# Cross-attention and a quantised FFN: keys from a transposed copy of the context, queries from a second layout of x normalised by ScalarE

## The reference

```python
def _L0_xattn_ref(Q, K, V):          # K = V = context, 16 heads of 16 columns
    q = Q.reshape(B, S, N_HEADS, D_K).transpose(0, 2, 1, 3)   # k and v likewise
    scores = jnp.einsum('bhqd,bhkd->bhqk', q, k) * scale      # scale = 1/4
    attn = jax.nn.softmax(scores, axis=-1)
    out = jnp.einsum('bhqk,bhkd->bhqd', attn, v)
    return out.transpose(0, 2, 1, 3).reshape(B, S, D_MODEL)
def fp4_linear(x, w):                # both quantised in blocks of 16, then x w^T
    return jnp.einsum('bsk,nk->bsn', fp4_quant_dequant(x), fp4_quant_dequant(w))
def _L0_ffn_ref(x, w_gate, w_up, w_down):
    h = jax.nn.silu(fp4_linear(x, w_gate)) * fp4_linear(x, w_up)
    return fp4_linear(h, w_down)
x = x + _L0_xattn_ref(_layernorm(x), ctx_1024, ctx_1024)
x = x + _L0_ffn_ref(_layernorm(x), L0_ffn_w_gate, L0_ffn_w_up, L0_ffn_w_down)
```

## Time and profile before

| | |
|---|---|
| time, 3 runs | median 542.06 us (539.32 to 543.23) |
| profiled execution | 543.02 us, span 541.2 us |
| busy | PE 498.4 (92%), PEld 398.7 (74%), DVE 453.1 (84%), ACT 360.9 (67%), POOL 270.0 (50%) |
| DMA | 40.63 MB, 75 GB/s on average |
| chain that ended last | PE 59%, DVE 21%, issue 11% |

### The profile page before, as it was taken

How to read it: one execution, slowest core, us unless ns; L and a number is a source line. 1 busy time by engine, 2 the same in 40 slices (tenths; PEclk the granted TensorE clock), 3 DMA queues, 4 the chain that set the end, 5 groups by cost and what they waited for, 6 DMA issues and landing times.

```text
span 541.2 us, 13897 instructions
## 1 busy us (share of the span) xinstructions
PE 498.4 (92%) x4105; PEld 398.7 (74%) x4132; DVE 453.1 (84%) x1175; ACT 360.9 (67%) x707; POOL 270.0 (50%) x391
## 2 busy tenths in 40 slices
PE   3788999999999999999886799999999999999996
PEld 2345666666666666655445699999999999999996
DVE  3688999999999999988554788888998888898764
ACT  3237888888888888877773456666566666656653
POOL 5214254445444345433415556676666666666543
PEclk9999999999999999999886899999999999999999
DMA  6758554454444554330000000000000000000000
GB/s 196 203 133 240 156 143 135 140 157 124 134 134 137 156 154 132 96 106 3 3 1 0 2 10 22 21 19 11 18 19 19 19 19 19 10 19 20 21 21 30
DMA packets 43799, 40.63 MB, mean 75 GB/s; under 512 B 4728, under 2 KB 43512, under 8 KB 43768
## 3 DMA queue, kind: packets, MB, share of 16 engines
q1 hardware_dynamic: 43768, 40.26, 26.2%
HBM read 10.55 MB, written 4.19 MB: 27 GB/s over the span
## 4 chain that ended last, share of the span: by engine, by line
PE 59%; DVE 21%; issue 11%; DMA 2%; POOL 2%; ACT 2%; DVEq 1%; SPq 0%; POOLq 0%; ACTq 0%
PE SC L1090 21%; DVE MF L682 12%; PE PV L1090 12%; PE MX L1023 4%; PE SC L1009 4%; PE PV L1041 4%; PE T L1115 4%; PE T L1120 2%; DVE stats L690 2%; DVE QN L703 2%; PE T L992 1%; DMA QS<-MT 1%; PE SC L1115 1%; PE T L955 1%; DVE MP L712 1%
## 5 line engine op out<-in xcount | busy, mean ns | idle before, releaser
L682 DVE TENSOR_REDUCE MF<-MX 128x2 f32<-128x512 f32 x256 | 167.5, 685 | 16.3 <-PE MX L1023 15.5
L535 ACT ACTIVATE P<-SC 128x512 f32<-128x512 f32 x256 | 142.7, 606 | 27.8 <-PE SC L1009 26.8
L1023 PE MATMUL MX<-KS,QS 96*128 96x256 bf16 x512 | 103.6, 287 | 6.7 <-DVE MF L682 2.9
L1009 PE MATMUL SC<-QS,KS 98*128 98x256 bf16 x512 | 100.2, 278 | 2.0 <-DMA QS<-MT 2.0
L484 POOL TENSOR_TENSOR HQ<-HN,hscale 128x704 f32<-128x704 f32 x31 | 43.2, 1393 | 61.4 <-DVE HN L839 61.4
L1041 PE MATMUL PV<-P,VA 128*32 128x256 f32 x1024 | 70.6, 394 | 2.7 <-ACT OT L544 0.8
L1009 PEld LDWEIGHTS SC<-QS,KS 98*128 98x128 bf16 x512 | 43.8, 98 | 36.3 <-ACT P L535 14.0
L614 ACT ACTIVATE HH<-T 128x768 fp32r<-128x768 f32 x31 | 25.2, 813 | 67.8 <-PE T L1115 67.8
L1090 PE MATMUL SC<-WH,XH 128*128 128x352 f32 x256 | 68.6, 350 | 0.0
L1023 PEld LDWEIGHTS MX<-KS,QS 96*128 96x128 bf16 x512 | 46.5, 100 | 29.3 <-DVE MF L682 19.0
L1090 PE MATMUL SC<-WH,XL 128*128 128x352 f32 x256 | 62.8, 327 | 0.0
(11 more groups left out here) (134 smaller groups left out, 1021.5 us busy)
## 6 DMA issues: line engine op xcount, KB each, us to landing
KS<-KP SPq DMA_DIRECT2D x96, 128.0 KB, 2.4
QS<-QP SPq DMA_DIRECT2D x96, 128.0 KB, 2.4
X<-in_x SPq DMA_DIRECT2D x16, 256.0 KB, 2.9
C<-in_ctx SPq DMA_DIRECT2D x16, 256.0 KB, 3.1
out<-OB SPq DMA_DIRECT2D x32, 128.0 KB, 1.7
W<-in_L_ffn_w_down SPq DMA_DIRECT2D x1, 704.0 KB, 5.7
W<-in_L_ffn_w_gate SPq DMA_DIRECT2D x1, 640.0 KB, 4.3
W<-in_L_ffn_w_up SPq DMA_DIRECT2D x1, 640.0 KB, 4.7
```

The lines of the kernel that those rows point to most:

```text
L535: nc.scalar.activation(P[g % 2][:, j, :, :], SC[h % 3][:, :, :], ACT.Exp, scale=0.25).then_inc(exp_done, 1)
L682: nc.vector.tensor_reduce(MF[st.slot(off, 2)][:, :, h:h + 1], MX[h % 2][:, :, :], AX.X, ALU.max, negate=True).then_inc(mx_done, 1)
L1009: last = nc.tensor.matmul(SC[h % 3][:, k, :], KS[r][0:ROWS, h, k * 128:(k + 1) * 128], QS[r][0:ROWS, h, :], start=True, stop=True)
L1023: last = nc.tensor.matmul(MX[h % 2][:, q, :], QS[r][0:PROD, h, q * 128:(q + 1) * 128], KS[r][0:PROD, h, :], start=True, stop=True)
```

## The change

Two further inputs are laid out before the launch: `x_p`, x with its columns by parity of the head, and `ctx_t`, the context transposed into the layout that the keys need. Both are loaded for each item beside x and the context (`load_first`), into rings of four buffers. The keys' parts no longer go through TensorE: ScalarE rounds the first part from the loaded tile, GpSimd subtracts it (KR), ScalarE rounds the second, GpSimd subtracts that and writes the third. The statistics are taken from the x_p tile, GpSimd makes a bias of mean and reciprocal root, and ScalarE normalises the tile in place with scale and bias. GpSimd's first work in a step is now the addition of the outputs to x. Many positions move.

```diff
-        QN = sb("QN", [128, QT, 2, DK, H // 2])
-        KN = sb("KN", [128, QT, 2, DK, H // 2])
+        QN = [sb(f"QN{r}", [128, QT, 2, DK, H // 2]) for r in range(RING)]
+        KT = [sb(f"KT{r}", [128, 512]) for r in range(RING)]
+        KR = sb("KR", [128, 512])
...
+            def load_first(b, r):
+                sp.dma_start(QN[r][:, :, :, :, :].rearrange("p q e d a -> p q (e d a)"),
+                             xp_d[:, bass.ds(b * QT, QT), :]).then_inc(first_loaded[r], 16)
+                sp.dma_start(KT[r][:, :], t_d[:, bass.ds(b, 1), :].rearrange("p a c -> p (a c)")).then_inc(first_loaded[r], 16)
+            def load_second(b, r):
+                sp.dma_start(C[r][:, :, :], c_d[:, bass.ds(b * QT, QT), :]).then_inc(loaded[r], 16)
...
                 for k_n, q_n, dst, parts, p, rows in ((1, 0, KS[0], KP[0], 0, (0, 3, 5)), (2, 0, KS[0], KP[0], 1, (1, 4)),
-                                                      (2, 1, QS[0], QP[0], 0, (0, 1, 2)), (3, 1, KS[0], KP[0], 2, (2,)),
+                                                      (3, 0, KS[0], KP[0], 2, (2,)), (3, 1, QS[0], QP[0], 0, (0, 1, 2)),
                                                       (3, 2, QS[0], QP[0], 1, (3, 4)), (3, 3, QS[0], QP[0], 2, (5,))):
-                    sp.wait_ge(k_out, k_n)
+                    sp.wait_ge(k_out if k_n < 3 else k_low, k_n if k_n < 3 else 1)
                     sp.wait_ge(q_out, q_n)
...
-            load(0, 0)
-            load(1, 1)
+            load_first(0, 0)
+            load_first(1, 1)
...
-            load(2, 2)
+            load_first(2, 2)
+            for b in range(2):
+                load_second(b, b)
...
-                    load(st.item(RING), st.slot(RING, RING))
+                    load_first(st.item(RING), st.slot(RING, RING))
+                    load_second(st.item(RING), st.slot(RING, RING))
                 if st.has(LEAD):
                     r = st.slot(LEAD, RING)
-                    sp.wait_ge(k_out, st.times(LEAD, 3, 3))
...
-                        load(3, 3)
+                        load_second(2, 2)
+                        load_first(3, 3)
                     if st.first == 2 - LEAD:
+                        load_second(3, 3)
...
-                if st.has(LEAD):
-                    r, rc = st.slot(LEAD, 2), st.slot(LEAD, RING)
-                    pool.wait_ge(loaded[rc], st.turn(LEAD, RING, 32))
-                    pool.wait_ge(k_tr, st.times(LEAD, 3))
-                    gate(pool)
-                    for q in range(QT):
-                        nc.gpsimd.tensor_scalar(KN[:, q, :, :, :], by_parity(C[rc][:, q, :]), 1.0, 0.0,
-                                                ALU.mult, ALU.add).then_inc(kn_ready, 1)
...
+                    r, rc = st.slot(LEAD, 2), st.slot(LEAD, RING)
+                    pool.wait_ge(k_out, st.times(LEAD, 2, 1))
+                    pool.wait_ge(k_low, st.times(LEAD, 1))
+                    gate(pool)
+                    nc.gpsimd.tensor_tensor(KR[:, :], KT[rc][:, :], KP[r][:, 0, :], ALU.subtract).then_inc(k_rest, 1)
+                if st.has(LEAD):
                     pool.wait_ge(stats_seq, st.times(LEAD, 4, 4))
                     gate(pool)
                     nc.gpsimd.tensor_scalar(ve[r][:, :], mv[:, :, 1], EPS, None, ALU.add).then_inc(ve_ready, 1)
-                    pool.wait_ge(ve_ready, st.times(LEAD, 1, 1))
+                    nc.gpsimd.tensor_scalar(nmean[:, :], mv[:, :, 0], -1.0, None, ALU.mult).then_inc(ve_ready, 1)
+                    pool.wait_ge(ve_ready, st.times(LEAD, 2, 2))
                     nc.gpsimd.tensor_tensor(rstd[r][:, :], ve[r][:, :], mhalf[:, :], ALU.pow).then_inc(rstd_ready, 1)
+                    pool.wait_ge(rstd_ready, st.times(LEAD, 1, 1))
+                    nc.gpsimd.tensor_tensor(qbias[r][:, :], nmean[:, :], rstd[r][:, :], ALU.mult).then_inc(qbias_ready, 1)
+                    pool.wait_ge(k_out, st.times(LEAD, 2, 2))
+                    gate(pool)
+                    nc.gpsimd.tensor_tensor(KP[r][:, 2, :], KR[:, :], KP[r][:, 1, :], ALU.subtract).then_inc(k_low, 1)
...
+            def key_part(st, n):
+                r, rc, rs = st.slot(LEAD, 2), st.slot(LEAD, RING), st.slot(LEAD - 2, RING)
+                if n == 0:
+                    act.wait_ge(first_loaded[rc], st.turn(LEAD, RING, 32))
+                    if st.first + LEAD >= 2:
+                        act.wait_ge(stacked[rs], st.turn(LEAD - 2, RING, 192))
+                    nc.scalar.activation(KP[r][:, 0, :], KT[rc][:, :], ACT.Copy).then_inc(k_out, 1)
+                else:
+                    act.wait_ge(k_rest, st.times(LEAD, 1, 1))
+                    nc.scalar.activation(KP[r][:, 1, :], KR[:, :], ACT.Copy).then_inc(k_out, 1)
+            def normalise(st, q):
+                r, z = st.slot(LEAD, 2), QN[st.slot(LEAD, RING)][:, q, :, :, :]
+                act.wait_ge(qbias_ready, st.times(LEAD, 1, 1))
+                nc.scalar.activation(z, z, ACT.Identity,
+                                     bias=qbias[r][:, q:q + 1], scale=rstd[r][:, q:q + 1]).then_inc(qn_ready, 1)
...
-                        for n, at in enumerate(((0, 3), (1, 1), (1, 2))):
-                            if (g, j) == at and st.has(LEAD):
-                                part_out(KP[st.slot(LEAD, 2)], TA, n, k_tr, k_out, st)
-                        if (g, j) == (0, 3) and st.has(GRID):
+                        if (g, j) == (0, 1) and st.has(LEAD):
+                            key_part(st, 0)
+                        if (g, j) == (0, 1) and st.has(GRID):
                             act.wait_ge(w_scaled, st.times(GRID, 1, 1))
                             act.wait_ge(w_grid, st.times(GRID, 2))
                             nc.scalar.activation(WC[:, :], wslice(st, GRID), ACT.Abs, scale=MAGIC).then_inc(w_abs, 1)
-                        if (g, j) == (0, 2) and st.has(-1):
+                        if (g, j) == (0, 3) and st.has(-1):
                             evacuate(st, -1, 1)
-                        for n, at in enumerate(((2, 1), (2, 3), (3, 3))):
+                        if (g, j) == (1, 1) and st.has(LEAD):
+                            key_part(st, 1)
+                        if (g, j) == (1, 2) and st.has(LEAD):
+                            for q in range(QT):
+                                normalise(st, q)
+                        for n, at in enumerate(((2, 2), (2, 3), (3, 3))):
                             if (g, j) == at and st.has(LEAD):
                                 part_out(QP[st.slot(LEAD, 2)], TB, n, q_tr, q_out, st)
-                        if (g, j) == (3, 1) and st.has(0):
+                        if (g, j) == (2, 2) and st.has(0):
                             evacuate(st, 0, 0)
...
             def statistics(st):
-                b, rc = st.item(LEAD), st.slot(LEAD, RING)
-                dve.wait_ge(loaded[rc], st.turn(LEAD, RING, 32))
+                rc = st.slot(LEAD, RING)
+                dve.wait_ge(first_loaded[rc], st.turn(LEAD, RING, 32))
+                dve.wait_ge(ve_ready, st.times(LEAD, 2))
                 for q in range(QT):
-                    nc.vector.bn_stats(stats[:, q, :], X1[:, bass.ds(b * (QT * D) + q * D, D)]).then_inc(stats_seq, 1)
+                    nc.vector.bn_stats(stats[:, q, :], QN[rc][:, q, :, :, :].rearrange("p e d a -> p (e d a)")).then_inc(stats_seq, 1)
             def aggregate(st):
                 for q in range(QT):
                     dve.wait_ge(stats_seq, st.times(LEAD, 4, 2))
                     gate(dve)
                     nc.vector.bn_aggr(mv[:, q, :], stats[:, q, :]).then_inc(stats_seq, 1)
-            def normalise(st, q):
-                r, b = st.slot(LEAD, 2), st.item(LEAD)
-                dve.wait_ge(rstd_ready, st.times(LEAD, 1, 1))
-                dve.wait_ge(q_tr, st.times(LEAD, 3))
-                nc.vector.tensor_scalar(QN[:, q, :, :, :],
-                                        by_parity(X1[:, bass.ds(b * (QT * D) + q * D, D)]),
-                                        mv[:, q, 0:1], rstd[r][:, q:q + 1],
-                                        ALU.subtract, ALU.mult).then_inc(qn_ready, 1)
...
-                        if (g, j) == (0, 1) and st.has(LEAD):
+                        if (g, j) == (0, 3) and st.has(LEAD):
                             statistics(st)
-                        if (g, j) == (0, 1) and st.has(LEAD):
                             aggregate(st)
                         if (g, j) == (1, 1) and st.has(SCALE):
                             weight_maxima(st)
-                        if (g, j) == (2, 3) and st.has(SCALE):
-                            weight_limits(st)
-                        if (g, j) == (3, 1) and st.has(SCALE):
-                            weight_inverses(st)
-                        if (g, j) == (1, 0) and st.has(LEAD):
-                            normalise(st, 0)
-                        if (g, j) == (1, 0) and st.has(LEAD):
-                            normalise(st, 1)
```

(45 more changed lines are left out.)

30 lines of the change are left out of this document (15 added, 15 removed).

## The result

The changed kernel takes 545.34 us (median of 17 runs, 541.82 to 548.50) where the kernel before takes 540.48 in the same session (17 runs). The ratio is 1.0083, interval 1.0064 to 1.0102: slower by 0.8%. That lies inside the range and inside "within 1%", but on the other side of zero than the 538.8 that I forecast. (The forecast started from a median of three runs, 542.06; from the 540.48 of 17 runs its -3.3 would give 537.2.) The profiled executions are 544.59 us (span 542.8) and 543.02 (541.2).

What follows compares the result with a forecast made beforehand. VectorE's list was taken to bound a full step, 15.12 us becoming 14.64. Terms -6.2 + 0.4 + 3.0 - 1.2 - 0.8 + 1.5 = -3.3 took the profile from 543.0 to 539.7, the median to 538.8 us; range 527 to 547.

Steps and rivals of the forecast that it cites:

- QN: Full step, VectorE: the QN pair of operations leaves its list, -0.83 us.
- MP: Full step, VectorE: the cast rounding the maxima no longer meets GpSimd's operations and falls from 0.53 to 0.17, -0.36 us.
- the collision: Full step, (3,0): VectorE's weight limits meet GpSimd's first operation on WC and wait, +0.55 us.
- The gaps at the PV blocks: Full step: VectorE idles 0.38 us at (1,2), (2,0) and (2,3), against 0.22 now, +0.16 us.
- TensorE: I count nothing: Full step: a flip and two subtractions leave TensorE, which waits for VectorE's maxima anyway; counted as 0.
- ScalarE: hidden: Full step: ScalarE's added normalisations cost at most +0.6 us, hidden in its idle time, 1.3 left.
- the step doesn't get shorter: Rival, full step: the gap passes to TensorE or ScalarE, the 6.2 us is missing, 545 us; chance 0.15.
- GpSimd and the late key part: Full step: subtractions take 1.3 us, bias ready 2.9 after the statistics' start; hidden with 0.7 us to spare.
- the rival of 552: Rival, full step: GpSimd's third key part comes late, TensorE waits 1.0 us for MT each step, 552 us; chance 0.09.
- Steps 13 and 14: The two steps after the full ones: -0.36 + 0.55 us each, +0.4 together.
- Step 15: Last step: WC's last piece moves to (2,3), so TensorE's lot 11 waits until about 281.8, +3.0 us (0 to +4).
- The start: Before the full steps: earlier first maxima -1.2 us, QN pair gone from step -1 -0.8, more loads +1.5.

Runs made afterwards that it cites:

- e7: The kernel before with WC rounded at (2,3) (in step 15 at (1,3)) and the weight limits at (3,0): 543.04 us, ratio 1.0042.
- e8: The kernel before with WC rounded at (2,3) (in step 15 at (1,3)) and the weight limits at (2,3) ahead of it: 540.11 us, ratio 0.9987.
- e2: The changed kernel with the weight limits at (2,3), ahead of the rounding of WC, instead of (3,0): 546.6 us, ratio 1.0078.
- e11: e9 with VectorE's weight limits at (2,3), ahead of the rounding of WC: 535.79 us, ratio 0.9916.
- e14: e11 with item 1's flip and two further query parts later in step -2, behind the first maxima: 537.65 us, ratio 0.9922.
- e1: The kernel before with two further loads of 256 KB per item, read by nobody, where the changed kernel has its additional loads: 546.58 us, ratio 1.0103.
- e3: The changed kernel with WC's last piece rounded at (1,3) instead of (2,3), in step 15 alone: 540.23 us, ratio 0.9992.
- e9: e3 with TensorE's second query part at (2,3) instead of (3,0) in every step: 538.3 us, ratio 0.9957.
- e13: e11 with the same bytes, but x, the up and down weights loaded behind the rows of maxima and contexts behind the stacks: 532.32 us, ratio 0.9844.
- e4: The changed kernel with item 0's row of maxima sent ahead of item 2's six key-stack DMAs, in step -1 only: 549.45 us, ratio 1.0168.
- e5: The changed kernel with x loaded at the end of its item's own step and the up and down weights in step 1: 547.58 us, ratio 1.0125.
- e12: e11 with x late, the contexts of items 1 and 2 behind step -1's stacks, up weights in step 1, down weights in step 3: 539.20 us, ratio 0.9958.

## Why the prediction was wrong in sign

*QN, MP and the collision: right in kind.* QN left. The cast fell by 0.27 and the subtraction behind it by 0.05 (246 to 192 ns): -0.32 for my -0.36. The collision lengthens the operation by 0.34, where I had 0.55. The limits begin 0.33 us after GpSimd's addition (129.30, 129.63), where I had 0.24, so 0.09 less of it is left. The rest is a mistake in my sum: the operation ends with GpSimd's, so its own 0.17 lie inside the 0.55 and don't come on top. I had used exactly this for the cast (0.53, -0.36) and not for the limits, whose term should have been 0.38. Both are worth less at the step's end, 0.20 and 0.23 (e7, e8). I had taken the cast from a single row; that one of 0.53 was a long one of eight with a mean of 0.44.

*The gaps at the PV blocks, +0.16: the mechanism was wrong, the size fits by chance.* VectorE's named waits disappeared. With -0.83, -0.32 and +0.34 the list would give 14.28; the step is 14.43, and it stays there when VectorE gets 0.35 shorter (e2). Without the 0.34 the list gives 13.94, and e11, with both bounds out of the way, runs at 14.02. "TensorE: I count nothing" and "ScalarE: hidden" failed. ScalarE did have idle time, but it is spent at the turns of the query parts, which TensorE makes at (3,0) and ScalarE needs at (2,3). The rival "the step doesn't get shorter" named that place, but it expected no gain, and the step got 0.66 shorter, 0.18 more than the 0.48 forecast; the collision's term makes that difference.

*GpSimd and the late key part:* the subtractions take 1.16 us each (I said 1.3), the bias is ready 3.0 us after the start of the statistics (2.9), and in nine steps TensorE waits once, 0.6 us, for a row of maxima. Right; the rival of 552 did not happen.

*Steps 13 and 14:* +0.35, predicted +0.4. *Step 15:* +4.5, predicted +3.0 with an end at +4. The place and the wait were right. I compared two absolute times, and so overlooked that the steps before the wait would end earlier than today. Lot 11 comes at 281.34, close to my 281.8; the wait lasts 4.14.

*The start: the step that failed and turned the sign.* I had -1.2 for first maxima that come sooner, -0.8 for QN, +1.5 for the loads, together -0.5. Measured is +4.7 at the mark of step 1, in spite of the gains of the steps up to there. With -0.5 in its place the profile would be 3.6 us faster than before, and the medians about equal. The first stack DMA did go out at 5.28 as worked out, but the first maxima came at 19.36, not sooner than 17.56, because item 1's flip stands ahead of them and waits for ScalarE's normalisation (17.30), which used to be a VectorE operation with nothing beside it. That costs nothing that the runs can tell (e14), but the -1.2 was not to be had either. The +1.5 was mis-sized: it should have been 5 to 6 (e1: +6.1 at this mark, +5.4 in the medians). I looked at how full the engines were, and there the argument should have been SP's order. Two more loads ahead of a row that everything waits for cost 1.0 us of issuing, out of the 2.3 by which the row goes out later; SP also reaches these loads 2.0 us later than before (30.37 against 28.32), and gets back some 0.7 us that it stood waiting before the key stack. And the row lands later behind loads and stack together: 4.83 to 6.87 us after its issue in the six profiles with the changed kernel's list (e2, e3, e9, e11, e14 and its own), 2.91 to 5.23 in the three with the list before. The stretch at the lower clock, about 1.4 us of the 4.7, is a third part that I had not thought of. e13 takes the whole loss back with the same bytes.

A single profile is a coarse measure of this: with the same or nearly the same start, step 1's mark comes at 68.79 and 69.44 in e2 and e3 (70.01), and at 64.72 and 66.60 in e7 and e8 (65.34). The loss stands clear of that spread, its size is good to about 1 us.

Sum of the profiled executions up to the FFN's first matmul: +4.7, -7.0, +0.35, +4.5, and 0.5 behind lot 11, +3.1 (293.01 to 296.08). The rest of the program is 1.5 us shorter in the changed kernel's profile, though its code is the same. Over the 17 profiles it takes either 248.2 to 248.5 us (six: the kernel before, e1, e7, e8, e9, e14) or 246.3 to 247.3 (eleven), and the granted clock of its first 20 us divides them in the same way: 0.78 to 0.80 in the six, 0.82 to 0.90 in the eleven. So this difference goes with the clock, not with the change.

Between the +3.1 and the +4.9 of the medians, 1.8 us are left that these profiles don't place. The clock is the nearest candidate here too. Over 102 executions of the kernel before, on record with the runs, the time follows the mean granted clock: 543.2 us for the ten at 0.978, 539.7 for the 21 at 0.990. The mean is 0.985 for them and 0.976 for the changed kernel's 17. At an equal clock the two are closer, though from different sessions: 545.5 against 543.2 at 0.978, 543.7 against 542.4 at 0.981. Whether the clock falls because of the new waits was not tested; that part of the loss stays open.

## What to carry to other kernels

When a change adds loads, don't ask only how full the DMA engines are: list what the issuing engine sends ahead of the one small transfer on which the chain hangs, in the start above all, and put the loads behind it, but not ahead of the next one of its kind (e4, e5 and e12 only handed the wait on). When three engines are all over 85% busy, taking time from the busiest one wins only down to the next chain; find that one's length first, and test edits in pairs, because each alone can show nothing. An operation moved within the last step of a loop needs its own look, since nothing behind it gives the time back.

## What I had not expected of the hardware

A DMA of 16 KB lands 2.9, 3.6 and 5.2 us after its issue in three profiles with two loads of 256 KB and six DMAs of 128 KB ahead of it (before, e7, e8), 4.8 to 6.9 us in six profiles with four loads and the same six (the changed kernel, e2, e3, e9, e11, e14), 2.4 with the four loads but not the six (e4), and 7.2 after six loads, the weights and three stacks (e4, issued 55.89). The same list thus varies by over 2 us from one execution to another, and the groups overlap at their ends. GpSimd's subtraction of 512 columns takes the same 1.16 us with a float32 or a bfloat16 result, both with a bfloat16 operand.
